# Four graph layers on one core: GpSimd adds x2 and makes a node's own message in the attention layer, and the softmax steps are interleaved

## What is computed

```python
x = layernorm(x + L0(x))   # per edge: exp(clip(k[src].q[dst])) weights v[src]; sums over dst
x = layernorm(x + L1(x))   # z = (1+eps)*x + sum x[src]; relu(z@W1+b1)@W2+b2; layernorm, relu
x = layernorm(x + L2(x))   # attention, below, with a loop from every node to itself
x = layernorm(x + L3(x))   # transformer convolution with edge features

def L2(x):                                    # per head, 8 heads of 32
    h = x @ W
    e = leaky_relu(a_src(h)[src] + a_dst(h)[dst], 0.2)      # loops included
    alpha = exp(e - segment_max(e)[dst]) / segment_sum(exp)[dst]
    out = segment_sum(h[src] * alpha, dst) + bias
    y = out + x
    return (y - mean(y)) / sqrt(var(y) + eps) * ln_w + ln_b
```

## Time and profile before

| | us |
|---|---|
| profiled execution | 5432.7 |
| its span | 5430.9 |
| PE busy | 4854.7 (89%) |
| DVE busy | 3946.8 (73%) |
| ACT busy | 2585.5 (48%) |
| POOL busy | 2142.3 (39%) |
| `nodes1` | about 1235 to 2607 |
| `nodes2` | about 2637 to 3990 |
| `nodes3` | about 4645 to 5431 |

### The profile page before, as it was taken

How to read it: one execution, slowest core, us unless ns; L and a number is a source line. 1 busy time by engine, 2 the same in 40 slices (tenths; PEclk the granted TensorE clock), 3 DMA queues, 4 the chain that set the end, 5 groups by cost and what they waited for, 6 DMA issues and landing times. The chain is left out here.

```text
span 5430.9 us, 97954 instructions
## 1 busy us (share of the span) xinstructions
PE 4854.7 (89%) x22356; PEld 3728.2 (69%) x22356; DVE 3946.8 (73%) x13675; ACT 2585.5 (48%) x6082; POOL 2142.3 (39%) x2171
## 2 busy tenths in 40 slices
PE   6999877778999999999788888888879999788888
PEld 3666544447888888888577777777756666577777
DVE  4333399997888888888389999999965555566666
ACT  2333344444555555555355655655531111355555
POOL 4666400006555555555245555554445555000000
PEclk8999955559999999999799999999989999899999
DMA  4444399983444444444356666666545555567665
GB/s 113 133 133 133 106 291 295 288 266 106 131 135 130 130 135 131 131 134 130 118 164 186 190 185 181 195 179 184 174 136 163 163 164 164 175 214 214 212 207 167
DMA packets 893392, 921.21 MB, mean 170 GB/s; under 512 B 116765, under 2 KB 855444, under 8 KB 893126
## 3 DMA queue, kind: packets, MB, share of 16 engines
q1 hardware_dynamic: 484174, 444.55, 28.2%
q10 hardware_dynamic: 333688, 318.57, 17.2%
q0 software_dynamic: 75264, 155.06, 10.1%
HBM read 632.48 MB, written 337.88 MB: 179 GB/s over the span
## 5 line engine op out<-in xcount | busy, mean ns | idle before, releaser
L1175 POOL DMA_INDIRECT nodes_near_rows<-hh_d,source_row x392 | 397.9, 1015 | 605.0 <-DVE nodes_weighted L1348 529.1
L767 PE MATMUL nodes_agg<-nodes_msg,nodes_hot 128*128 128x264 f32 x784 | 410.0, 678 | 135.8 <-issue 92.6
L846 POOL DMA_INDIRECT nodes_near_rows<-x_d,nodes_cur x392 | 425.7, 1086 | 236.3 <-POOL nodes_cur L841 169.2
L1491 POOL DMA_INDIRECT edges_xg<-x_d,edge_rows x392 | 371.5, 948 | 258.6 <-PE edges_x_ps L1517 176.2
L432 POOL DMA_INDIRECT edges_xg<-in_x,edge_rows x392 | 370.5, 945 | 256.3 <-PE edges_t_ps L448 135.0
L767 PEld LDWEIGHTS nodes_agg<-nodes_msg,nodes_hot 128*128 128x128 f32 x784 | 229.2, 323 | 316.2 <-issue 275.2
L649 ACT ACTIVATE nodes_x<-nodes_outer_rows,nodes_outer_shift,nodes_outer_rstd 128x256 f32<-128x256 f32 x784 | 425.6, 593 | 19.6 <-DVE nodes_outer_shift L642 14.4
L1733 PE MATMUL nodes_agg<-w_s,nodes_xT 128*128 128x256 f32 x1568 | 412.2, 386 | 1.9 <-ACT nodes_xT L1750 1.9
L854 POOL TENSOR_TENSOR nodes_xb<-nodes_xin,row_L_gnn_b 128x512 f32<-128x512 f32 x196 | 248.1, 1266 | 380.6 <-DVE nodes_inner_rows L880 380.4
L959 PE MATMUL nodes_h_ps<-w_h,nodes_x2T 128*128 128x272 f32 x1568 | 392.2, 393 | 6.7 <-ACT nodes_x2T L1036 6.7
L969 PE MATMUL nodes_hid_ps<-nodes_zT,w_a 128*128 128x256 f32 x1568 | 372.4, 381 | 0.7 <-ACT nodes_zT L1045 0.7
(11 more groups left out here) (209 smaller groups left out, 12468.5 us busy)
## 6 DMA issues: line engine op xcount, KB each, us to landing
nodes_xin<-x_d SPq DMA_DIRECT2D x588, 256.0 KB, 3.1
nodes_msg<-msg_d SPq DMA_DIRECT2D x784, 132.0 KB, 3.5
x_d<-nodes_x ACTq DMA_DIRECT2D x392, 256.0 KB, 3.2
hh_d<-nodes_hh ACTq DMA_DIRECT2D x196, 264.0 KB
x_d<-nodes_y ACTq DMA_DIRECT2D x196, 256.0 KB
nodes_hin<-hh_d SPq DMA_DIRECT2D x196, 256.0 KB, 3.8
nodes_xin<-in_x SPq DMA_DIRECT2D x195, 256.0 KB
out<-nodes_y ACTq DMA_DIRECT2D x195, 256.0 KB, 3.2
```

The lines of the kernel that those rows point to most:

```text
L767: last = nc.tensor.matmul(agg[ring(u, 2)][:, h, 0:D + H], hot[:, ring(u, 4), h, :], msg[:, r, h, :], start=True, stop=True)
L846: gp.indirect_dma_start(out=near_rows[:, r, h, :], out_offset=None, in_=x1_d, in_offset=bass.IndirectOffsetOnAxis(ap=cur[:, r, h:h + 1], a ...
L1175: gp.indirect_dma_start(out=near_rows[:, u % NR, h, :], out_offset=None, in_=hh_d, in_offset=bass.IndirectOffsetOnAxis(ap=source_row[:, 2 ...
L1491: gp.indirect_dma_start(out=xg[:, c % 8, k, :], out_offset=None, in_=x3_d, in_offset=bass.IndirectOffsetOnAxis(ap=edge_rows[:, c, k:k + 1] ...
```

## The change

**x2 and ln_b.** `nodes1` now stores x2 + ln_b: GpSimd adds it (`x2b`, lag 11, behind `xb` in its queue), and ScalarE issues the store at lag 13 instead of 11. So that the sum is right, ln_b is taken off the bias once, in `prepare`.

**nodes2.** GpSimd makes `own`: ScalarE copies own_ps + 1 to `own_share` (lag 15), GpSimd multiplies `hin` by it (lag 16) and in the next step adds x2 (now with ln_b) to it (lag 17, semaphore `based`). In its body the order is: gathers, add, product. TensorE's x2 matmuls go, and its sum moves to lag 18 and waits for `based`; `xb` goes, and VectorE's `outer_rows` adds `xin`. `weighted` moves to lag 16, still read by the gathers' wait, and all that follows to one lag more. The edge product is done 12 steps later (`LATER`): its transposes, copy, product, copy and store stand beside the one-hot work of a later unit. VectorE zeroes the slots of `near_rows` one by one in the first 16 steps. The rings `xin` (10), `weighted`, `own` (4) and `hot` (19) are larger. The instructions of the four softmax steps no longer stand at the end of a step but between the norm's, and a chain step waits for the one before it only where it needs it (`marked` gives `mark` and `settle`).

**nodes3.** GpSimd issues the loads of the windows.

```diff
+                link(nc.vector.tensor_tensor(b3[:, 0:D], b3[:, 0:D], rows["L2_gnn_ln_b"][0:3, :], ALU.subtract))
...
+                    u = at(11)
+                    if u:
+                        gp.wait_ge(outer["normed"], num(u) + 1)
+                        if had(u, 4):
+                            gp.wait_ge(x2_out[ring(u, 4)], turn(u, 4) * 16)
+                        gp.tensor_tensor(x2b[:, ring(u, 4), :, :], x2[:, ring(u, 4), :, :], both(rows["L2_gnn_ln_b"]), ALU.add)\
+                          .then_inc(x2_biased, 1)
+                run_steps(gp, UNITS, 11, body)
...
-                            act.wait_ge(x2_out[ring(u, 4)], turn(u, 4) * 16)
+                            act.wait_ge(x2_biased, num(u) - 3)
...
-                        act.wait_ge(outer["normed"], num(u) + 1)
-                        act.dma_start(unit_rows(x2_d, u), x2[:, ring(u, 4), :, :]).then_inc(x2_out[ring(u, 4)], 16)
...
+                        act.wait_ge(x2_biased, num(u) + 1)
+                        act.dma_start(unit_rows(x2_d, u), x2b[:, ring(u, 4), :, :]).then_inc(x2_out[ring(u, 4)], 16)
...
-        NR, HR, WR = 16, 6, 3
+        NR, HR, XR, WR, HOT, LATER = 16, 6, 10, 4, 19, 12
...
-                gp.memset(near_rows[:, :, :, :], 0.0).then_inc(zeroed, 1)
-                gp.wait_ge(zeroed, 1)
-
                 def body(s, at):
                     u = at(0)
                     if u is not None:
-                        if u >= NR:
+                        if u < NR:
+                            gp.wait_ge(zeroed, u + 1)
+                        else:
                             gp.wait_ge(weighed, u - NR + 1)
                         for h in range(2):
                             gp.indirect_dma_start(out=near_rows[:, u % NR, h, :], out_offset=None, in_=hh_d,
                                                   in_offset=bass.IndirectOffsetOnAxis(ap=source_row[:, 2 * u + h:2 * u + h + 1], axis=0),
                                                   bounds_check=NPAD - 1, oob_is_err=False).then_inc(near_in[u % NR], 16)
-                    u = at(18)
-                    if u is not None:
-                        gp.wait_ge(x_in[u % HR], u // HR * 16 + 16)
+                    u = at(17)
+                    if u is not None:
+                        gp.wait_ge(own_done, u + 1)
+                        gp.wait_ge(x_in[u % XR], u // XR * 16 + 16)
+                        gp.tensor_tensor(own[:, u % WR, :, :], own[:, u % WR, :, :], xin[:, u % XR, :, :], ALU.add).then_inc(based, 1)
+                    u = at(16)
+                    if u is not None:
+                        gp.wait_ge(own_known, u + 1)
+                        gp.wait_ge(h_in[u % HR], u // HR * 16 + 16)
                         if u >= WR:
-                            gp.wait_ge(outer["filled"], u - WR + 1)
-                        gp.tensor_tensor(xb[:, u % WR, :, :], xin[:, u % HR, :, :], both(rows["L2_gnn_ln_b"]), ALU.add)\
-                          .then_inc(biased, 1)
-                run_units(UNITS, 18, body)
+                            gp.wait_ge(inner["filled"], u - WR + 1)
+                        gp.tensor_tensor(by_head(own[:, u % WR, :, :]), by_head(hin[:, u % HR, :, :]),
+                                         over_head(own_share[:, u % 4, :, :]), ALU.mult).then_inc(own_done, 1)
+                run_units(UNITS, 17, body)
...
-                    u = at(17)
+                    u = at(18)
                     if u is not None:
                         to = agg[u % 4]
-                        pe.wait_ge(x_in[u % HR], u // HR * 16 + 16)
                         pe.wait_ge(weighed, u + 1)
-                        pe.wait_ge(own_done, u + 1)
+                        pe.wait_ge(based, u + 1)
                         if u >= 4:
                             pe.wait_ge(outer["filled"], u - 3)
                         for h in range(2):
                             cols = to[:, h * D:(h + 1) * D]
-                            nc.tensor.matmul(cols, hot[:, u % 18, h, :], weighted[:, u % WR, h, :], start=True, stop=False)
-                            nc.tensor.matmul(cols, ident[:, :], xin[:, u % HR, h, :], start=False, stop=False)
+                            nc.tensor.matmul(cols, hot[:, u % HOT, h, :], weighted[:, u % WR, h, :], start=True, stop=False)
                             nc.tensor.matmul(cols, ones3[:, :], bias3[:, 0:D], start=False, stop=False)
                             last = nc.tensor.matmul(cols, ident[:, :], own[:, u % WR, h, :], start=False, stop=True)
                         last.then_inc(inner["filled"], 1)
...
-                ve.wait_ge(zeroed, 1)
 
                 def body(s, at):
-                    u = at(19)
+                    if s < NR:
+                        nc.vector.memset(near_rows[:, s, :, :], 0.0).then_inc(zeroed, 1)
+                    masks, scores, tops, shares = (g // GU if g is not None and g % GU == 0 else None
+                                                   for g in (at(10), at(11), at(12), at(13)))
...
-                    u = at(15)
-                    if u is not None:
-                        w = 2 * u % (2 * GU)
-                        ve.wait_ge(own_summed, u + 1)
-                        ve.wait_ge(h_in[u % HR], u // HR * 16 + 16)
-                        if u >= WR:
-                            ve.wait_ge(inner["filled"], u - WR + 1)
-                        less_one = own_ps[:, w * H:(w + 2) * H].rearrange("p (h w) -> p h w", h=2)
-                        nc.vector.scalar_tensor_tensor(by_head(own[:, u % WR, :, :]), over_head(less_one), 1.0, by_head(hin[:, u % HR, :, :]),
-                                                       ALU.add, ALU.mult).then_inc(own_done, 1)
...
+                        mark(nc.vector.tensor_tensor_scan(sm["run"][0:n, :], sm["join"][0:n, 0:P], score_ps[0:n, 0:P], -BIG, ALU.add, ALU.max))
...
+                    g = tops
+                    if g is not None:
+                        n = of_group(g) * H
+                        settle()
+                        mark(nc.vector.tensor_tensor_scan(sm["top"][0:n, ::-1], sm["join"][0:n, 1:P + 1][:, ::-1], sm["run"][0:n, ::-1], -BIG,
+                                                          ALU.add, ALU.max))
...
+                    u = at(16)
+                    if u is not None:
+                        share = head_columns(share_ps, of_group(u // GU))
+                        ve.wait_ge(share_turned, u // GU + 1)
+                        if u >= WR:
+                            ve.wait_ge(inner["filled"], u - WR + 1)
+                        nc.vector.tensor_tensor(by_head(weighted[:, u % WR, :, :]), by_head(near_rows[:, u % NR, :, 0:D]),
+                                                over_head(share[:, 2 * u % (2 * GU):2 * u % (2 * GU) + 2, :]), ALU.mult).then_inc(weighed, 1)
...
+                        nc.vector.tensor_tensor(outer["rows"][:, u % 4, :, :], in_halves(agg[u % 4]), xin[:, u % XR, :, :], ALU.add)\
...
+                    u = at(15)
+                    if u is not None:
+                        w = 2 * u % (2 * GU)
+                        act.wait_ge(own_summed, u + 1)
                         if u >= 4:
+                            act.wait_ge(own_done, u - 3)
+                        nc.scalar.activation(own_share[:, u % 4, :, :], own_ps[:, w * H:(w + 2) * H].rearrange("p (h w) -> p h w", h=2),
+                                             ACT.Copy, bias=1.0).then_inc(own_known, 1)
...
+            @blk.gpsimd
+            def _(gp):
+                for g in range(GROUPS_OF_UNITS):
+                    load_pairs(gp, sm, g)
...
-                    g = at(0)
-                    if g is not None and g % GU == 0:
-                        load_pairs(act, sm, g // GU)
```

320 lines of the change are left out of this document (188 added, 132 removed).

## The result

The changed kernel takes 5769.09 us (median of 4 runs, 5766.8 to 5773.18), against 5423.08 us before (median of 4 runs, the three above among them): a ratio of 1.0637, with a 95% interval of 1.0619 to 1.0656. It is 6.4% slower, where 2.7% was forecast with a range that ended at 5710 us. The sign was right, the size was not.

The account below looks back on a forecast made before the run. It took TensorE to bound nodes1, VectorE and the TensorE-ScalarE ring nodes2. nodes1 +2, nodes2's start -27, its steps +202, nodes3 -30 make +147 on 5432.7, 5580 profiled; 5573 us timed, range 5370 to 5710.

Parts of the forecast that it names:

- nodes1: Stage nodes1: GpSimd's second add may cost VectorE up to 1.27 us a step, covered by 1.33 idle; +2 us.
- The start: Start of nodes2: short fills of near_rows and the edge product 12 steps later give -27 us, bounds -15 and -40.
- The ring: nodes2: TensorE's sum waits for GpSimd's add, queued behind gathers waiting for nodes_weighted; two steps take at least 11.94 us.
- out of the middle: nodes2: TensorE at 1.2 GHz after idling, up to 0.6 us a step, left to the range, not the middle forecast.
- VectorE against GpSimd: nodes2: GpSimd's add and product block VectorE instructions; 60.5 us a group, 7.56 a step, +202 us over 180 steps.
- 4.7 and 9.4: nodes2: forecast us of the first two of four regular steps after the softmax steps, short and long in turn.
- tops 6.6 (`nodes_first` waits): nodes2: the third softmax step of a group was to take 6.6 us, with nodes_first held up by GpSimd.
- W + 0.8: nodes2: outer norm's reciprocal after a long step, 0.8 us after W, the moment VectorE ends nodes_weighted; step 4.1 to 4.7.
- 4.1 and 10.0: nodes2: forecast us of the last two of a group's eight steps, the second long because nodes_hot is held.
- nodes3: Stage nodes3: pair loads moved from ScalarE to GpSimd end TensorE's wait; -30 us, bounds -35 and -15.
- 8.2 us a step: nodes2: upper bound of the step, +317 us over 180 steps; with it the third rival gives 5690 us.
- the third: Rival, worse: clock at half through most long steps, or GpSimd's product well over 1.28 us; 5690 us, chance 0.20.

Follow-up runs that it names:

- all three: The changed kernel with GpSimd's add and product ahead of the gathers, shares' transpose at lag 15, softmax at the end of VectorE's step: 5371.37 us, 0.9804 of before.
- kernel with the add ahead: The changed kernel with only GpSimd's add of x2 and product in nodes2 moved ahead of the two gathers: 5668.78 us, 1.0328 of before.

## Why the prediction was wrong, step by step

- **nodes1** held. VectorE loses nearly what I said could be lost: its busy time rose from 811 to 985 us in 1000, 1.22 us a step against 1.27, with `nodes_scaled` and `nodes_affine` at 0.77 and 0.79 us instead of 0.48 and 0.46. The wait before `nodes_z` went from 1.31 us a step in the mean to 0.09, and TensorE stays busy at 1.00. The cover was just enough and was used up.
- **The start** gave -40, more than the -27 taken, at the end of its bounds.
- **The ring** was found, its place, its order and its first half to 0.01 us (4.44). Its second half was mis-sized: 5.73 instead of 4.16 us in the pass shown, since TensorE comes out of that wait at 1.2 GHz. I had seen that clock in the earlier trace rows and left it "out of the middle". That is a wrong step of its own: a ring that makes TensorE wait can make it slow where the ring needs it. In all, TensorE's busy time in `nodes2` was the same as before (1145 and 1144 us) with four matmuls a unit less.
- **VectorE against GpSimd** was right in kind: the steps I forecast at 4.7 and 9.4 took 4.77 and 8.97, the scores step 7.75 for 8.1. The masks step took 8.97 for 7.2 and the shares step 8.69 for 10.4, which nearly cancel. The product took 1.05 us, not 1.31.
- **The step that failed most** is "tops 6.6 (`nodes_first` waits)". It took 12.45 us, and `nodes_first` 0.22. In it VectorE waited 3.16 us for the outer root and 2.57 for the scores, and `nodes_hot` took 1.2 us more than usual. I had the root early after a long step ("W + 0.8"); it came 3.96 us after W, since TensorE had worked at 1.2 GHz through the step before. And I reckoned the softmax steps by VectorE's own instructions and GpSimd's stretch, and did not ask where on TensorE's queue the scores that the moved scan wants are made. They are last in its step, and that step is late by ring and clock.
- **The second that failed**: the last two steps of a group, "4.1 and 10.0" for 14.1, took 16.65 us (11.60 and 5.05). That is the share's bank: with the transpose one step later they came out at 4.04 and 10.53 in one group. The code had all the parts: weighted to 16, share's transpose at 14. I checked the new waits that the diff adds, and not the old wait whose one side had moved.
- Together: tops 5.85 and the last two 2.55 us more, the other steps 0.6 less, group 68.3 us against 60.5 forecast. 7.8 us in 22 groups is 172 of the missing 196 us; `nodes3` has 22, and the small terms nearly cancel.
- **nodes3** gave -8 instead of -30. The wait before `nodes_score_ps` is gone but for the first (46.5 us in 23 times to 21.3 in one), as forecast. It wasn't worth that, since TensorE's own work became longer: 689.0 us busy instead of 670.3 for the same 3578 matmuls, 18.7 of the 22 us. Its clock was 0.98 to 1.00 in the six stretches of 100 us behind the first before, and is 0.95 in all six now. One of each, of before and of after (4847.4 and 5192.8 us):

```profile
4847.40:4947.40 100.00, 85.22 (x464) 69.05 (x463) 65.57 (x263) 55.06 (x116) 0.00 (x0) 1.00 0.71 217
```

```profile
5192.80:5292.80 100.00, 90.83 (x475) 74.59 (x476) 66.01 (x268) 54.06 (x116) 11.67 (x24) 0.95 0.70 213
```

What made the clock fall is not settled; no run tried it.
- **The range**: its upper end of 5710 lay a little above the sum with 8.2 us a step, 5690. The measured 8.54 is outside because each unknown was bounded by itself, while waits in one chain add to each other. Of the rivals the third, which had the clock low through the long steps and a chance of 0.20, came nearest.

## What to carry to other kernels

When an instruction is moved by a step, write down for every semaphore it signals and every buffer it reads who waits for it, old waits first: a consumer that stayed where it was is the wait that no diff line shows. An operation that feeds the critical engine must not stand in a queue behind a wait for that engine's result; turning two lines of GpSimd's step round was worth 3% here. And where a change makes several waits at once, undoing one shows only part: only with all three did the rest of the change turn out to be a gain, of 2%.

## What the hardware showed that I had not expected

- A VectorE instruction that is caught waits for all of GpSimd's tensor operations that follow each other, even if it stood before the first began: `nodes_keep`, at 2992.39 us, with the add starting at 2992.99, took 3.03 us instead of 0.29, to just after the end of the product at 2995.26 us (kernel with the add ahead). It began 0.60 us before the add, 0.43 us into the gather ahead of it. It was not the gather that held it: in the same trace, near the start of the stage, it began just as far into a gather behind which GpSimd had nothing to do for 3.32 us, and took 0.29. VectorE, then GpSimd:

```profile
2730.32 0.29 DVE L1390 TENSOR_TENSOR nodes_keep<-nodes_target 128x127 f32<-128x127 f32 x1
...
2729.90 1.15 POOL L1209 DMA_INDIRECT nodes_near_rows<-hh_d,source_row  x1 [0.30 <-issue]
2734.36 1.04 POOL L1200 TENSOR_TENSOR nodes_own<-nodes_hin,nodes_own_share 128x512 f32<-128x512 f32 x1 [3.32 <-ACT nodes_own_share L1523]
...
2992.39 3.03 DVE L1390 TENSOR_TENSOR nodes_keep<-nodes_target 128x127 f32<-128x127 f32 x1
...
2991.96 1.00 POOL L1209 DMA_INDIRECT nodes_near_rows<-hh_d,source_row  x1 [0.30 <-issue]
2992.99 1.28 POOL L1193 TENSOR_TENSOR nodes_own<-nodes_own,nodes_xin 128x512 f32<-128x512 f32 x1
```

  What counted was how soon an add followed. In the traces of both kernels and of nine runs, instructions of these kinds (`nodes_hot`, `nodes_keep`, `nodes_join`, `nodes_first`, `nodes_score`, the scan of totals, `nodes_share`) began 577 times inside a gather with an add directly behind it: the 106 that began 0.75 us or more before the add's listed start took at most 0.29 us, the 471 that began 0.74 us or less before it took 1.33 or more. So the hold begins some 0.75 us before the add's start in the profile; why is not shown.
- The clock follows the waits in the mean: 0.93 in a steady stretch of `nodes2` before, 0.80 after, 0.93 again with all three edits. Such a wait costs once as idle time and once more as matmuls at 1.19 us for 0.60. Not every wait does: in the kernel with the add ahead TensorE waited 2.71 us before 2997.87 us, and its next matmuls took 0.58 us (four small ones) and 0.60 (a pair of the sum), as at the upper level.
- The same code of `edges0` took 606 to 608 us in ten of the traces and 645 to 652 in the four of another chip, while `nodes1` of the changed kernel took 1414 to 1415 us in all of its traces. A comparison of stages over chips holds only for stages shown to be alike.
